# Graph attention layer: the second load of x put ahead of the store of head sums, a shift moved on GpSimd, and 64-wide rows copied by ScalarE

## The reference, cut to what matters

```
xp    = x @ W                        # three heads of 128
ex    = exp(leaky(a_src[row] + a_dst[col] + a_edge) - max of the node)
agg   = segment_sum(ex / denom * xp[row], col)      # edges, and each node's own row
h     = x + agg @ lin_W + bias
x3    = layernorm(x + (layernorm(h) * ln_g + ln_b))
next  = x3 @ L3_W1                   # 64 wide, the first product of the fourth layer
```

## Time and profile before

| what | value |
|---|---|
| median of 3 runs | 10529.21 us (10516.9 to 10536.39) |
| the profiled execution's own time | 10513.06 us |
| its span in the profile | 10510.6 us |
| VectorE busy, share of the span | 8002.5 us, 76% |
| GpSimd busy | 7840.4 us, 75% |
| TensorE matmul busy | 6426.3 us, 61% |
| ScalarE busy | 5904.7 us, 56% |

### The profile page before, as it was taken

How to read it: one execution, slowest core, us unless ns; L and a number is a source line. 1 busy time by engine, 2 the same in 40 slices (tenths; PEclk the granted TensorE clock), 3 DMA queues, 4 the chain that set the end, 5 groups by cost and what they waited for, 6 DMA issues and landing times. The chain is left out here.

```text
span 10510.6 us, 142293 instructions
## 1 busy us (share of the span) xinstructions
PE 6426.3 (61%) x32436; PEld 5258.3 (50%) x32436; DVE 8002.5 (76%) x33105; ACT 5904.7 (56%) x13869; POOL 7840.4 (75%) x7586
## 2 busy tenths in 40 slices
PE   6037666667774666667755666786457675654444
PEld 3026655555664666667755666674235443432222
DVE  8359899956667999999988888655558777874444
ACT  0026577767776999978957777432125443432222
POOL 7767688867776888766637777687777777878887
PEclk8569988878886555578868888665558765765555
DMA  3999888832223777634424555464336443432222
GB/s 114 330 299 314 286 289 289 289 123 75 76 74 121 234 236 235 207 126 139 142 87 160 173 175 177 145 172 120 92 104 183 143 116 99 139 111 65 63 65 60
DMA packets 1019500, 1694.47 MB, mean 161 GB/s; under 512 B 304877, under 2 KB 535080, under 8 KB 1018594
## 3 DMA queue, kind: packets, MB, share of 16 engines
q1 hardware_dynamic: 782752, 1361.06, 38.8%
q0 software_dynamic: 175936, 218.82, 9.3%
q10 hardware_dynamic: 59970, 105.49, 2.9%
HBM read 988.03 MB, written 707.78 MB: 161 GB/s over the span
## 5 line engine op out<-in xcount | busy, mean ns | idle before, releaser
L1351 POOL DMA_INDIRECT g_got<-scaled,row_src x2352 | 2230.1, 948 | 751.5 <-issue 631.8
L903 DVE SCALAR_TENSOR_TENSOR g_sums<-g_got,first,g_sums 128x128 f32<-128x128 f32 (+3 forms) x3136 | 871.6, 278 | 1159.5 <-DMA g_got<-scaled,row_src 1148.4
L299 PE MATMUL g_a_p_z<-sb_L_gnn_W,g_a_u_t 128*128 128x128 f32 (+3 forms) x2574 | 603.8, 373 | 592.5 <-DVE g_sums L1073 197.4
L1186 ACT COPY g_a_u_t<-g_a_p_t 128x512 f32<-128x512 f32 (+3 forms) x495 | 224.8, 454 | 1222.2 <-PE g_a_p_t L1138 637.3
L907 DVE SCALAR_TENSOR_TENSOR g_sums<-g_sums,cont,g_got 128x128 f32<-128x128 f32 (+3 forms) x3128 | 881.3, 282 | 0.0
L299 PEld LDWEIGHTS g_a_p_z<-sb_L_gnn_W,g_a_u_t 128*128 128x128 f32 (+1 forms) x2574 | 443.1, 245 | 759.9 <-ACT g_a_u_t L1186 398.3
L299 PE MATMUL g_bb_p_z<-sb_L_gnn_W,g_bb_u_t 128*128 128x128 f32 (+2 forms) x4302 | 755.8, 336 | 84.7 <-DVE g_bb_z L1078 77.0
L299 PEld LDWEIGHTS g_bb_p_z<-sb_L_gnn_W,g_bb_u_t 128*128 128x128 f32 x4302 | 676.0, 237 | 135.6 <-issue 108.9
L1186 ACT COPY g_bb_u_t<-g_bb_p_t 128x1024 f32<-128x1024 f32 (+2 forms) x294 | 233.6, 795 | 774.6 <-PE g_bb_p_t L290 774.1
L2475 POOL DMA_INDIRECT gb_got<-x,row_src x392 | 404.8, 1033 | 242.1 <-POOLq L178 138.1
L458 POOL DMA_INDIRECT f_got<-in_x,idx_dst x396 | 463.2, 1170 | 139.8 <-issue 120.1
(11 more groups left out here) (496 smaller groups left out, 23955.6 us busy)
## 6 DMA issues: line engine op xcount, KB each, us to landing
raw<-gb_u SPq DMA_DIRECT2D x98, 768.0 KB, 3.9
xs<-f_o ACTq DMA_DIRECT2D x97, 516.0 KB
f_x<-in_x ACTq DMA_DIRECT2D x97, 512.0 KB
g_bb_own<-in_x SPq DMA_DIRECT2D x97, 512.0 KB
wide<-g_bb_o SPq DMA_DIRECT2D x97, 512.0 KB
g_bb_own<-wide SPq DMA_DIRECT2D x97, 512.0 KB
g_bb_res<-in_x SPq DMA_DIRECT2D x97, 512.0 KB
x<-g_bb_o SPq DMA_DIRECT2D x97, 512.0 KB
```

Source lines behind the costliest of these rows:

```text
L299: last = nc.tensor.matmul(dst_psum[0:p, q * g * width:(q * g + n) * width], turned_tile[0:n * k, q * P:q * P + p], weight[0:n * k, 0:n * w ...
L903: nc.vector.scalar_tensor_tensor(out=self.firsts, in0=new, scalar=first[:, col], in1=self.firsts, op0=ALU.mult, op1=ALU.add).then_inc(run_ ...
L1186: last = nc.scalar.copy(to, source)
L1351: pool.indirect_dma_start(got[b.s4][:, c * row:(c + 1) * row], None, table, bass.IndirectOffsetOnAxis(ap=index[:, b.n * CH + c:b.n * CH + ...
```

## The change

In `attention_pass`, SyncE's list has `load_again` ahead of `store_sums`, and `store_sums` comes one step later (lag 2 for 1). GpSimd's list has `add_beta` ahead of `gather_firsts`. In `attention_gather_pass`, the copy of `p_g` to `g_s` leaves VectorE's list and becomes the last stage of ScalarE's, at the same lag, as a `copy_out` with the same waits and the same signal.

```diff
-                g = split(self.g_s[b.s], p, j, H1)
-                if self.a:
-                    nc.vector.tensor_tensor(g, split(self.p_g, p, j, H1), window_rows(inv, b, H1), ALU.mult
-                                            ).then_inc(m.finished, 1)
-                else:
-                    nc.vector.tensor_copy(g, split(self.p_g, p, j, H1)).then_inc(m.finished, 1)
+                nc.vector.tensor_tensor(split(self.g_s[b.s], p, j, H1), split(self.p_g, p, j, H1), window_rows(inv, b, H1),
+                                        ALU.mult).then_inc(m.finished, 1)
+
+            def copy_out(self, b):
+                p, j = self.r.pj(b)
+                m, act = self.m, nc.scalar
+                act.wait_ge(m.scored, b.n + 1)
+                if b.after(2):
+                    act.wait_ge(m.stored_b[b.s], b.pair * DMA)
+                nc.scalar.copy(self.g_s[b.s][0:p, 0:j * H1], self.p_g[0:p, 0:j * H1]).then_inc(m.finished, 1)
...
-                                       (n.stats_2, 5, NB), (n.factors_1, 3, NB), (n.out_rows, 8, NB)])
+                                       (n.stats_2, 5, NB), (n.factors_1, 3, NB)])
...
-                                       (n.evacuate_out, 7, NB), (n.normalise_2, 6, NB)])
+                                       (n.evacuate_out, 7, NB), (n.normalise_2, 6, NB), (n.copy_out, 8, NB)])
...
-                        pipeline(pool, [(gather, 0, NBE), (weigh_own, 1, NBA), (gather_firsts, 1, NBA), (n.add_beta, 4, NBA)])
+                        pipeline(pool, [(gather, 0, NBE), (weigh_own, 1, NBA), (n.add_beta, 4, NBA), (gather_firsts, 1, NBA)])
...
-                        pipeline(sp, [(load, 0, NBA), (store_sums, 1, NBE), (load_again, 2, NBA), (n.store, 7, NBA),
+                        pipeline(sp, [(load, 0, NBA), (load_again, 2, NBA), (store_sums, 2, NBE), (n.store, 7, NBA),
```

## The result

The changed kernel takes 10611.49 us (median of 4 runs, 10603.25 to 10619.66) against 10525.06 for the kernel before (4 runs): a ratio of 1.0081, 95% interval 1.0064 to 1.0099. It is slower by 86 us; 258 were forecast.

The account below looks back on a forecast made before the run. VectorE was taken as the busiest engine in both passes. A 303 us loss in the attention pass less 45 us from the copy made +258, so 10529 + 258 = 10787 us, range 10640 to 10850.

Parts of the forecast that it names:

- That `weigh_own` would be released by the end of `add_own`, GpSimd being ready: Attention pass: loads go out a step earlier, so `add_own` decides; GpSimd needs 9.63 us, under VectorE's 10.68.
- That it would meet VectorE's operations with two inputs in SBUF: Attention pass: GpSimd's multiplications and `add_beta` hold `nmr` of `factors_2`; 303 us lost over 92 steps.
- the end that the prediction gave for no stall: Attention pass: if GpSimd held nothing up, 97 steps would each lose 0.55 us of waits, 53 us gained.
- A floor of 10.68 us for the step: Attention pass: VectorE's shortest step, `rows` to `rows`, against a mean step of 11.23 us.
- the full one: Attention pass: `nmr` held through all GpSimd operations until `add_beta` ends, 3.84 us a step; chance 0.60.
- the one row with this meeting: First steps of the attention pass before the change: `nmr` took 2.96 us, ending 0.03 us after `add_beta`.
- the forecast's step: Attention pass: 10.68 us plus the 3.84 us stall, a step of 14.52 us.
- The first rival: Attention pass: VectorE gets in between two GpSimd operations; 2.73 us stall, 201 us lost, 10685 us in all; chance 0.20.
- 45 us from the copy: Gather pass: moving the copy to ScalarE gains 0.50 us in each of some 90 steps.
- the 8.92 forecast: Gather pass: ScalarE's chain of 8.35 us plus a copy of 0.57 us becomes the step's bound.
- upper end of 58: Gather pass: the gain if the copy hides wholly, 97 steps of 0.60 us.
- The other rivals: Attention pass: no meeting since the load still lands late (10431 us, chance 0.11); new order does nothing (10484, 0.06).

Follow-up runs that it names:

- e4: The changed kernel with GpSimd waiting for the end of `add_own` ahead of its four gathers instead of behind them: 10459.42 us, ratio 0.9928 to the kernel before.
- e8: The changed kernel with `weigh_own` and `add_beta` cut to 8 columns of one row in most blocks: 10442.02 us against 10527.19 for the kernel before.
- e10: The changed kernel; GpSimd waits for the end of `add_up`, then runs two gathers, `weigh_own`, `add_beta` and two gathers: 10814.79 us (one run).
- e6: The kernel before with only the copy moved to ScalarE, placed ahead of `evacuate_out`: 10464.08 us against 10527.19, ratio 0.9943.
- e3: The changed kernel with the store of sums back at lag 1, behind the repeated load: 10466.31 us, ratio 0.9938 to the kernel before.
- e5: The changed kernel; GpSimd waits for the end of `add_own`, then runs two gathers, `weigh_own`, `add_beta` and two gathers: 10763.38 us (one run).
- e9: The changed kernel; GpSimd issues one gather, waits again for `add_x` just ahead of `weigh_own`, three gathers after `add_beta`: 10517.26 us against 10528.98 before.

## Why the prediction was wrong

- *That `weigh_own` would be released by the end of `add_own`, GpSimd being ready:* right; 230.1 us of its waits moved there.
- *That it would meet VectorE's operations with two inputs in SBUF, and that this outweighs the gain:* right; e4 and e8 take the meeting away and gain 74 and 85 us, the copy's part included. In e4 the attention pass alone goes from 1157.2 to 1104.2: 53 us, the end that the prediction gave for no stall.
- *A floor of 10.68 us for the step:* right; e4 and e8 run at it.
- *"I take the full one, since the one row with this meeting shows it whole": this step failed.* The stall is 1.89 us by the three holds (1.85 by the step, 12.53 - 10.68), not 3.84. The earlier trace rows showed a run of operations that followed a gather without a wait; in the changed kernel GpSimd waits just ahead, and then VectorE gets its turn after each operation. So the row was read rightly, but it came from a step in which GpSimd had not stood still, while the prediction itself had GpSimd stand and wait for `add_own` in every step. e10, without that wait, has about the forecast's step: 14.8 us against 14.52. With the measured step, 92 x (12.53 - 11.23) = 120 us in place of 303; the pass shows 117.
- *The first rival* was the mechanism, and was given 0.20. Its price (2.73) was too high: `gain` ran straight behind `nmr` in the same turn (at 6008.51 in the step shown above) instead of waiting for the second multiplication, so that `add_x` was held by the second and not the third. It also left out the second `nmr`, held 0.57 us beside `add_beta`.
- *45 us from the copy:* half. At full clock the step is 8.8 us, a little better than the 8.92 forecast. But the mean step fell by 0.35 instead of 0.50 us, and the pass's end, from the last `rows` to the last copy, grew from 38 to 50 us. What I counted as hidden, TensorE behind the copy, was not; e6, which releases it earlier, brings the pass from 960.8 to 901.0 us: 60 us, about the upper end of 58.
- *The other rivals:* `weigh_own` staying with its load is what e3 brings back, and it is faster, as that rival said; the order had an effect.

## What to carry to other kernels

Before a load or a store is moved up, look at what its lateness was keeping apart: here a late load had set GpSimd's work beside VectorE operations that it does not disturb. Where GpSimd works on SBUF beside VectorE operations with two inputs there, use a wait to choose the moment at which the GpSimd work starts (e4). Read the price of a meeting from a row in which GpSimd came to it in the same way, with or without a wait just ahead. When a copy moves to another engine, place it so that it releases the engine behind it as early as before.

## What the runs showed that I had not expected

A VectorE operation with two inputs in SBUF that comes during one of several back-to-back GpSimd operations was held through all that were left (4.14 us in e10, 3.53 in e5) when GpSimd ran into them from a gather, but for the one step of e10 shown above, and by one (0.57 to 0.72 us in the changed kernel, 0.65 in e9) when GpSimd had waited on a semaphore just ahead. The whole kernels e10 and e9, which differ in where GpSimd waits and in how many gathers it issues ahead of `weigh_own` (two and one), lie 298 us apart: 10814.79 and 10517.26 (one run each).
